# Three blocks for the last three layers replaced by one program of slots, newest sequence first

## The reference

```
x = x + L2_ffn(norm(x))
    # base = n @ W.T + b;  t = n @ A (8 experts of rank 16)
    # routing = softmax(mean(n[107:127]) @ router_W.T + router_b), one row for each sequence
    # + 2 * (routing * t) @ B
x = x + L3_xattn(key=ctx, value=ctx, query=norm(x))
    # sim[c, d] = ctx[c] . n[d] * 128**-0.5, softmax over c;  out[c] = sum over d of sim[c, d] ctx[d]
x = x + L3_ffn(norm(x))
    # scores = softmax(n @ router.T + bias), 64 experts; w = the top 8 of them
    # n * sum(w) + w @ expert_bias
```

## Time and profile before

| | |
|---|---|
| median of the runs | 1915.94 us (1914.8 to 1918.7) |
| profiled execution: its time, its span | 1916.45 us, 1914.7 us |
| busy: PE, DVE, ACT, POOL | 1710.4, 1207.4, 796.3, 965.1 us |
| mean granted TensorE clock | 0.936 |
| first product of "f2" starts | 1738.27 us |

### The profile page before, as it was taken

How to read it: one execution, slowest core, us unless ns; L and a number is a source line. 1 busy time by engine, 2 the same in 40 slices (tenths; PEclk the granted TensorE clock), 3 DMA queues, 4 the chain that set the end, 5 groups by cost and what they waited for, 6 DMA issues and landing times. The chain is left out here.

```text
span 1914.7 us, 27377 instructions
## 1 busy us (share of the span) xinstructions
PE 1710.4 (89%) x8880; PEld 1428.4 (75%) x8880; DVE 1207.4 (63%) x2310; ACT 796.3 (42%) x2510; POOL 965.1 (50%) x977
## 2 busy tenths in 40 slices
PE   3799965689999999999999999999999999977566
PEld 2688854478888887888788788888888888866455
DVE  5376655556767777666778665576656655545554
ACT  2188830134444444444444444444444544441121
POOL 2033310066666768666567675566756656622002
PEclk9889987699999999999999999999999999998665
DMA  3000010122222213112122232222222322201011
GB/s 128 23 1 1 0 38 1 46 78 61 61 56 56 78 56 83 56 56 56 50 61 67 68 87 61 56 67 72 72 67 73 83 67 67 83 6 39 10 43 45
DMA packets 56928, 104.21 MB, mean 54 GB/s; under 512 B 7904, under 2 KB 8416, under 8 KB 56672
## 3 DMA queue, kind: packets, MB, share of 16 engines
q1 hardware_dynamic: 55072, 98.86, 17.9%
q10 hardware_dynamic: 1728, 3.75, 0.5%
HBM read 100.49 MB, written 2.10 MB: 54 GB/s over the span
## 5 line engine op out<-in xcount | busy, mean ns | idle before, releaser
L83 POOL TENSOR_TENSOR a_w_lo<-a_raw,a_w_hi 128x512 fp32r<-128x512 f32 x186 | 240.7, 1294 | 14.9
L68 PE MATMUL ps<-a_wo_hi,a_oT_lo 128*128 128x512 f32 x544 | 225.7, 415 | 6.4 <-DVE a_oT_lo L83 4.9
L865 POOL CAST a_w_hi<-a_raw 128x512 fp32r<-128x512 f32 x186 | 115.0, 618 | 202.4 <-PE ps L70 202.4
L70 PE MATMUL ps<-a_wo_hi,a_oT_hi 128*128 128x512 f32 x544 | 214.0, 393 | 0.0
L69 PE MATMUL ps<-a_wo_lo,a_oT_hi 128*128 128x512 f32 x544 | 212.5, 391 | 0.0
L872 POOL TENSOR_TENSOR a_probs<-a_probs,a_total 128x512 f32<-128x512 f32 x128 | 135.6, 1060 | 148.2 <-DVE a_total L1296 144.4
L68 PE MATMUL ps<-a_xT_hi,a_w_lo 128*128 128x512 f32 x512 | 204.7, 400 | 5.2 <-DVE a_w_lo L83 5.2
L70 PE MATMUL ps<-a_xT_hi,a_w_hi 128*128 128x512 f32 x512 | 204.1, 399 | 0.0
L69 PE MATMUL ps<-a_xT_lo,a_w_hi 128*128 128x512 f32 x512 | 203.9, 398 | 0.0
L1133 ACT ACTIVATE a_v_hi<-ps 128x128 fp32r<-128x128 f32 x128 | 35.5, 278 | 360.8 <-PE ps L981 360.8
L83 POOL TENSOR_TENSOR a_wo_lo<-a_raw,a_wo_hi 128x512 fp32r<-128x512 f32 x128 | 165.6, 1294 | 10.3
(11 more groups left out here) (371 smaller groups left out, 4690.6 us busy)
## 6 DMA issues: line engine op xcount, KB each, us to landing
a_raw<-in_L_wq SPq DMA_DIRECT2D x128, 256.0 KB, 2.6
a_raw<-in_L_wo SPq DMA_DIRECT2D x128, 256.0 KB, 2.6
a_raw<-in_L_wkv SPq DMA_DIRECT2D x64, 256.0 KB, 2.6
x<-in_x ACTq DMA_DIRECT2D x8, 256.0 KB, 9.1
setup_raw<-in_cT SPq DMA_DIRECT2D x4, 512.0 KB, 7.3
a_raw<-in_L_main SPq DMA_DIRECT2D x8, 256.0 KB, 3.0
a_c_raw<-in_context SPq DMA_DIRECT2D x2, 1024.0 KB, 7.4
out<-x SPq DMA_DIRECT2D x8, 256.0 KB, 2.0
```

The source lines that it names most:

```text
L68: pe.matmul(out, lhs_lo, rhs_hi, start=start, stop=False)
L70: return pe.matmul(out, lhs_hi, rhs_hi, start=False, stop=stop)
L83: return eng.tensor_tensor(out_lo, value, hi.bitcast(F32), ALU.subtract)
L865: pool.tensor_copy(hi, r).then_inc(s["chunk_hi"], 1)
```

## The change

The three blocks are replaced by one, `last_layers`. Its work on a sequence is cut in 22 stages, and `slots()` gives all engines one common order: stage n of sequence i stands in slot 4 i + n, and within a slot the smaller n, that is the newer sequence, comes first. Every engine walks this list and does its own part of each stage. `last_layers` keeps single statistics tiles for each norm, normalises on ScalarE (`normed_x`, before it was VectorE), takes the reciprocal roots one column at a time on GpSimd, and splits the context on GpSimd. What was one instruction for eight sequences (routing, softmax, top 8) is now one for each. The weights of the layer-2 FFN (four main pieces, side, up) are loaded and split within `two_attentions`, at its steps 97 to 107, in tiles that outlive it (`kept_on`).

```diff
     if T == 22:
         after.append(("U", 0, 0))
+    if T in (97, 99, 101, 103):
+        after.append(("M2", 0, (T - 97) // 2))
+    if T == 105:
+        after.append(("S2", 0, 0))
+    if T == 107:
+        after.append(("U2", 0, 0))
     return before, after
...
+            elif kind == "M2":
+                eng.wait_ge(s["q_mm"], HALF_ITEMS * 3)
...
+PER_BATCH = 4
+STAGES = "N2a N2b T2 M2 Ra Rb RT U2 N3a N3b T3 Sa Sb Sc O3 N4a N4b T4 La Lb WT U4".split()
+
+def slots():
+    for m in range(PER_BATCH * (B - 1) + len(STAGES)):
+        for n in range(m % PER_BATCH, len(STAGES), PER_BATCH):
+            i = (m - n) // PER_BATCH
+            if 0 <= i < B:
+                yield STAGES[n], i
+
+def last_layers(nc, C, A, out, kept_on):
...
+        @block.sync
+        def _(sp):
+            sp.dma_start(bias_row[:, :], A["L2_ffn_b"].partition_broadcast(128)).then_inc(s["rows"], 16)
+            sp.dma_start(route_row[:, :], A["L2_ffn_router_b"].partition_broadcast(128)).then_inc(s["rows"], 16)
+            sp.dma_start(row3[:, :], A["L3_ffn_router_bias"].partition_broadcast(128)).then_inc(s["rows"], 16)
+            for i in range(B):
+                sp.dma_start(c_raw[:, blk(i, D)], A["context"][i]).then_inc(s["context"], 16)
+            for i in range(B):
+                sp.wait_ge(s["added4"], i + 1)
+                sp.dma_start(out[i], x_of(i)).then_inc(s["stored"], 16)
...
+        @block.gpsimd
...
+                elif stage == "M2":
+                    if i == 0:
+                        pool.wait_ge(s["context"], 16 * B)
+                    pool.tensor_copy(c_s[0][:, at], c_raw[:, at]).then_inc(s["c_hi"], 1)
...
+        @block.tensor
...
+                elif stage == "M2":
+                    pe.wait_ge(s["lo2"], i + 1)
+                    wait_from_one(pe, s["added2"], i)
+                    matmul_tiles(pe, bank_main, tiles(xT[2], S), tiles(main, D)).then_inc(s["main"], 1)
+                    wait_from_one(pe, s["rT_lo"], i)
+                    matmul_tiles(pe, bank_side[:, 0:SIDE1], tiles(xT[2], S), tiles(side, SIDE1)).then_inc(s["side"], 1)
...
+                elif stage == "T4":
+                    wait_from_one(pe, s["wT_lo"], i)
+                    turn(4, i)
...
+        @block.vector
...
+                elif stage == "M2":
+                    dve.wait_ge(s["main"], i + 1)
+                    dve.wait_ge(s["biased"], i + 1)
+                    dve.tensor_tensor(x_of(i), x_of(i), bank_main, ALU.add).then_inc(s["added2"], 1)
...
+                elif stage == "U2":
+                    dve.wait_ge(s["up2"], i + 1)
+                    dve.scalar_tensor_tensor(x_of(i), bank_up, 2.0, x_of(i), ALU.mult, ALU.add).then_inc(s["sum2"], 1)
...
+                elif stage == "Sa":
+                    dve.wait_ge(s["s3"], i + 1)
+                    link(dve.tensor_reduce(most[:, :], bank_s[:, 0:S], AX.X, ALU.max))
...
-        two_attentions(nc, C, A)
-        ffn_phase(nc, C, "f2", MeanRoute, A["L2_main"], A["L2_side"], A["L2_up"], 2.0, bias=A["L2_ffn_b"],
-                  extra=[A["L2_ffn_router_b"]])
-        attention_transposed(nc, C, A["context"])
-        bias_experts(nc, C, A["L3_router"], A["L3_ffn_router_bias"], A["L3_ffn_expert_bias"], out)
+        attentions_to_end(nc, C, A, out)
```

More of the change, by code:

```diff
@@ L682, in chunks_of_step, with two_attentions @@
         after.append(("U", 0, 0))
+    if T in (97, 99, 101, 103):
[4 more added lines that the diff above has]
+        after.append(("U2", 0, 0))
     return before, after
-def two_attentions(nc, C, A):
+def two_attentions(nc, C, A, kept_on):
+    first_xT, side, up = kept_on
     with ExitStack() as ctx:
         ph = Phase(nc, ctx, "a")
-        R_ = [ph.split(f"xT{h}", KT * HALF * S) for h in (0, 1)]
+        R_ = [first_xT, ph.split("xT1", KT * HALF * S)]
         raw = [ph.sb(f"raw{k}", KT * SIDE1) for k in range(N_RAW)]
@@ L707, in columns_of @@
         def columns_of(c):
-            return KT * SIDE1 if c[0] == "S" else CHUNK
+            return KT * SIDE1 if c[0] in ("S", "S2") else CHUNK
         def source_of(c):
@@ L717, in source_of @@
                 return A["L1_up"]
+            if kind == "M2":
+                return A["L2_main"][:, h * D:(h + 1) * D]
+            if kind == "S2":
+                return A["L2_side"]
+            if kind == "U2":
+                return A["L2_up"]
             layer, g = u // LAYER_UNITS, group_of(u)
@@ L804, in home @@
                 return tuple(head(x, (HQ * u + h) % N_O, D) for x in o_ring)
-            if kind == "M":
+            if kind in ("M", "M2"):
                 return tuple(head(x, h, D) for x in R_[u])
-            if kind == "S":
+            if kind in ("S", "S2"):
                 return tuple(x[:, :] for x in side)
-            if kind == "U":
+            if kind in ("U", "U2"):
                 return tuple(x[:, :] for x in up)
@@ L821, in wait_home_free @@
                 eng.wait_ge(s["q_mm"], HALF_ITEMS * (u + 1))
+            elif kind == "M2":
+                eng.wait_ge(s["q_mm"], HALF_ITEMS * 3)
+            elif kind == "S2":
+                eng.wait_ge(s["f_side"], B)
+            elif kind == "U2":
+                eng.wait_ge(s["f_up"], B)
             elif kind in W_KINDS:
@@ L1468, with attentions_to_end @@
+def attentions_to_end(nc, C, A, out):
+    with ExitStack() as ctx:
+        ph = Phase(nc, ctx, "k")
+        kept_on = ph.split("xT0", KT * HALF * S), ph.split("side", KT * SIDE1), ph.split("up", D)
+        two_attentions(nc, C, A, kept_on)
+        last_layers(nc, C, A, out, kept_on)
 HD0 = 16
```

489 lines of the change are left out of this document (271 added, 218 removed).

## The result

The changed kernel takes 1939.51 us in the median of four runs (1928.5 to 1944.68), the kernel before 1917.19 beside it (1914.8 to 1918.7). The ratio is 1.0102, with a 95% interval of 1.0073 to 1.0132: slower by 1.0%, 22 us. Forecast were 1935.0 in a range of 1905 to 1959. The sum came out 4.5 us off, and partly by luck: two of its terms were wrong, in opposite directions.

A forecast was written before the change was run, and what follows sets the result against it. The three last blocks (189.7 us) were bound by heads without TensorE plus dense TensorE work at 0.50 clock. Periods 207.6 and start 1.2 make 208.8, so +19.1 on 1916.45: 1935.5, less 0.5 for the median: 1935.0 us, range 1905 to 1959.

The forecast's parts named there:

- The start of the program and the context load: At the new program's head: 1.2 us to start, and 0 (bounds 0 and 3) for waiting on the context pieces.
- The six pieces: Casting and splitting six layer-2 FFN weight pieces on GpSimd in the second attention layer: 0 us, bounds 0 and 11.5.
- The rival with 0.06: The six weight splits are late in the attention: up to 11.5 us on top, 1946 us; chance 0.06.
- Attentions unchanged: The attentions end at 1725.03 us as in the kernel before; a later end would show the forecast wrong.
- Part A: In a full period, VectorE's chain after the newest scores, with TensorE idle but for two small pieces: 7.4 us.
- The clock: TensorE starts low after idleness; narrow products don't raise it, 4.6 us of wide products in main do.
- part B: In a full period, TensorE's gapless run from norm 4's transposes through the router product, at the low level: 7.65 us.
- the second rival: TensorE gets the high level already in the expert product, transposes and layer-3 product: period 19.5, 1903 us; chance 0.17.
- The periods: The new program's 12.5 periods of four slots, each laid out alone: full ones 23.5 us, all together 207.6 us.
- point of decision: A mean full period under about 20.6 us (19 us less) makes the second rival decide for faster.
- The sum: New program 208.8 against 189.7 us, so +19.1 on 1916.45: 1935.5, and 1935.0 us for the median.
- the four signs: Wrong if period under 21, VectorE over 70% busy mid-program, router product at 0.11 apiece, or attentions ending after 1725.

The follow-up runs named there:

- kernels 2, 3 and 5: Six weight pieces: added to the kernel before (1926.1 us); moved in the changed kernel to steps 99 to 119 (1945.4 us) or 97 to 117 (1932.3 us).
- kernel 7: The changed kernel timed again without any edit: 1939.6 us, ratio 1.0099 to the kernel before.
- kernel 1: The changed kernel with the oldest sequence first in every slot: 1920.0 us, ratio 1.0008 to the kernel before.
- kernel 9: The changed kernel with unread 512-column products where TensorE waits, from period 5 on: 1913.7 us, ratio 0.9982 to the kernel before.
- kernel 6: The changed kernel with the oldest sequence first and the six weight pieces at steps 97 to 117: 1915.8 us, ratio 0.9969 to the kernel before.
- kernel 10: kernel 6 with unread 512-column products before router products and, for the last three sequences, before top-8 weight steps: 1892.8 us, ratio 0.9864 to the kernel before.
- kernel 12: The kernel before with unread 512-column products in its three last blocks: 1905.1 us, ratio 0.9919 to the kernel before.
- kernel 11: The changed kernel with the oldest sequence first in three slots of four, the fourth staying newest first: 1956.3 us, ratio 1.0198 to the kernel before.

## Why the prediction was right, and where it was not

*The start of the program and the context load, 1.2 and 0:* right; the gap is 1.23, and the first three periods took 39.5 us (1745.15 to the first scores at 1784.68), forecast 39.2.

*The six pieces, 0 with bounds 0 and 11.5:* wrong. They cost 7.3 us, 5.7 of waits and 1.6 of clock (kernels 2, 3 and 5). The step that failed was to read GpSimd's 202.4 us of idle time as room for them. That was a sum over 186 casts; ahead of the probabilities of every fourth item the queue had none. The rival with 0.06 had the right mechanism.

*Attentions unchanged, 1725.03:* they ended at 1743.92; besides the pieces 11.6 us of low clock, which differ between executions of the same program (kernel 7), though perhaps not wholly. The forecast took one execution's clock as the program's.

*Part A, 7.4:* right; from the scores (1836.11) to the transposes of norm 4 (1843.03) it is 6.9, made of the pieces it was said to be made of.

*The clock, and part B, 7.65 low and main 4.6 more low:* wrong. TensorE was low for 5.8 us from the transposes on and then high, ahead of router and main. Transposes, the expert product and the layer-3 product raised it together, which the second rival (0.17) said; I had let the narrow products of the earlier trace rows decide for a mix that has six wide ones in it, although one of the two rises that were read from the earlier trace rows, the one of 3.0 us, itself began with four transposes. The Trainium skill (TensorE: Matmul & The Clock Gate, Part 1, What you observe) has the rate rise partway through a run of 128-column products. Of the mix that held here; of the 96 products of 128 columns in the earlier trace rows alone it did not, which stayed at 0.50 for 20.7 us. The full period of 20.38 us shows the sizes: part A 6.9, from the transposes to main 7.0 (7.65 forecast), main 2.9 (4.9), side, up, scores and read 3.5 (3.5).

*The periods:* full 20.4 instead of 23.5; periods 3 to 7 took 92.2 us instead of 108.9. The rival's 19.5 was nearer. By its point of decision, 20.6, a period of 20.4 meant faster, and the tail was slower: periods 8 to the end took 65.7 instead of 59.5 (8 and 9: 33.8 instead of 32.3, the last three: 31.9 instead of 27.2), at 0.50 as laid out, so the tail came to 198.7 instead of 208.8, and 189.7 before. Which step of the last three was too short in the forecast isn't worked out.

*The sum:* +7.3 and +11.6 that weren't in it, -10.1 in the tail: 27.9 us between the spans of the two profiled executions where 19.1 were forecast, and 22.3 between the medians. The sign, and the reason for it (a rigid order in which VectorE and TensorE take turns), stand: kernel 1 takes 20 us out of the tail with nothing but the order. That 1935 came so near is luck: 10.1 us too much in the tail stood against 7.3 of pieces and some low clock. Of the four signs that were to show it wrong, three came: a period under 21, router products at 0.11, and attentions that end later. The fourth (VectorE over 70% busy) did not, at 55% in a full period.

## What to carry to other kernels

Where engines walk a common list of stages in order, put work that needs nothing new (the oldest data) ahead of work that waits for the newest result: turning the order round was worth 20 us in 199. Idle time summed over a queue isn't room for more work; look whether the run of pieces in front of what another engine waits for has a gap. And where TensorE waits often and briefly, its unread wide products can be faster than its silence, so count the clock of a stretch, not only its instructions, before a pipeline with many short gaps replaces blocks with few long ones.

## What was not expected of the hardware

- The clock's price: 148 unread products made a kernel 26 us faster, with 0.92 as the mean granted clock over the tail in place of 0.67 (kernel 9); the last 50 us of kernel 6, with TensorE busy for 60% of them, ran at 0.50, and 28 us of the same stretch in kernel 10 at 1.00.
- Narrow products alone stayed at 0.50 for 22 us; with filler ahead of the block and two wide products ahead of each twelve they ran at 1.00 (kernel 12).
- The same 76 rows of TensorE took 14.0 us in a full period at 0.75, 17.5 at 0.64 with as much idle time in it, only cut in four waits in place of two (kernel 11).
- The same program gets low-clock stretches at some executions and not at others, worth up to 9 us in the first 430: the runs of kernel 1 go from 1911.6 to 1931.6, those of the kernel before beside it from 1915.2 to 1928.0. A difference of 1% between two single profiles can be this alone. Matching the same instructions in both traces shows where it arises, and only more executions whether it belongs to the change.
